# Macaron block: the attention's first layer norm takes its statistics from a summing add and a square, and one normalisation moves behind the exponentials

## The chip, the cores and the metric

The kernel runs on one core of one Trainium2 chip. The metric is the device time of one execution in microseconds (us). A core has TensorE (matmuls, PE in the profile), VectorE (DVE), ScalarE (ACT), GpSimd (POOL) and SyncE (SP), which here only issues DMAs. Each engine works through its own list in order and waits on semaphores for the others.

## The reference

The input x is (8, 1024, 512) in f32: 8192 rows of 512. Three residual blocks follow each other:

```python
x = x + 0.5 * ffn(layernorm(x), gate_w, gate_b, w1, w2)
x = x + attn(layernorm(x), Wq, bq, Wk, bk, Wv, bv, Wo, bo)
x = x + 0.5 * ffn(layernorm(x), gate_w, gate_b, w1, w2)

def layernorm(x):   # over the 512 columns
    return (x - mean(x)) / sqrt(var(x) + 1e-5)

def attn(x):        # 16 heads of 32
    q, k, v = exp(x @ Wq.T + bq), exp(x @ Wk.T + bk), x @ Wv.T + bv
    kv = cumsum(k[:, :, :, None] * v[:, :, None, :], axis=1)
    num = einsum('zsD,zsDd->zsd', q, kv)
    den = sum(q * cumsum(k, axis=1), axis=-1, keepdims=True)
    return (num / den) @ Wo.T + bo
```

ffn is a mixture of 32 experts: for each batch the gate picks the 8 rows with the highest softmax weight for every expert, merges them into one token, passes it through the expert (512 to 2048, gelu, 2048 to 512), and adds the output back at the picked rows.

## The kernel before

Rows are handled in 64 tiles of 128 rows, eight tiles to a batch. The program has three parts in time: the gate and the first ffn's 32 experts (to about 1020 us), the attention over the 64 tiles (to about 1840 us), and the second ffn's experts with the final add. During the first experts the products of the normalised input with Wq, Wk and Wv are computed ahead and stored in DRAM (p_scratch), scaled by the row's standard deviation. What the first ffn adds to a row is a combination of few expert outputs; its share in the three products is then added by a small matmul (a combination matrix MS against OS).

The change is in the attention part. Every engine's list there is a loop over n from -2 to 72, written out by hand (attention_sp, attention_pe, attention_act, attention_dve, attention_pool); in step n the tile n is live, tile m = n + 1 is prepared, and tiles n - 1 and n - 2 are finished. The steps of one tile, with the lines of the profile:

- TensorE computes for tile m four products into PSUM banks 4 to 7: the ffn's share in key, query, value (banks 4 to 6), and the ffn output itself (bank 7), semaphore s_c.
- VectorE makes X1 = x + 0.5 * bank 7 (L1133, s_x1), then adds banks 4 to 6 to the key, query and value products loaded from DRAM (PB; three adds, in the page at the helper's line L266; s_tk, s_tq, s_tv). Then it computes X1's statistics (L1139), aggregates them to mean and variance (L1141) and adds epsilon (L1143, s_x1ve).
- GpSimd raises variance plus epsilon to the power -0.5 (L1198, RS).
- ScalarE takes the exponential of the key part with scale RS (L1072), casts it to its high half KH (L1078), takes the exponential of the query part (L1080) and scales the value part (L1083). OS and the products ahead are centred, so the mean isn't needed here.
- GpSimd computes the key's low half KL (L1201), multiplies the query by exp(bias) (L1204), adds the output bias to X1 (L1207).
- TensorE adds the running sum over keys (UPTO times KH and KL, bank 2); VectorE multiplies it by the query (PR, at L266), reduces it per head (L1173) and inverts it (L1176); GpSimd multiplies the query by it (L1210).
- In the next step TensorE transposes key and query (L262); ScalarE copies them out (KT, L1060; QT, L1063); TensorE computes the scores of four heads per bank in banks 4 to 7, which have to be free for it; VectorE masks them (ST, L266); TensorE computes the attention's sums into bank 3 (s_av); ScalarE copies them out (AT, L1101) and casts the high half (ATH, L1104); GpSimd computes the low half (ATL, L1227).
- One step later TensorE does the output projection from ATH and ATL into bank 0 (s_op); VectorE adds X1 to it and sums the rows (X2, L1165, SX2); ScalarE squares it with an accumulator (L1092, SQ2); GpSimd makes scale and shift from the sums (L1217, L1220, L1222).
- One step later still ScalarE normalises X2 into XN3 (L1067, s_x2n); TensorE transposes it and ScalarE copies it (L1097); every fourth tile the gate's logits follow (ScalarE L1112). X2 is one buffer: the add L1165 of the next tile waits for XN3 of this one and for the store of X2 to DRAM.
- From tile 10 on, in every batch of eight steps, VectorE and ScalarE do the top-k of a batch (step 8k + 2: L324, L329; 8k + 3: L342, L350), TensorE and ScalarE merge its rows (L358, L365, L379), VectorE ends the merge (L392).

In step n ScalarE's order is: KT copy, QT copy, XN3 of tile n - 2, then for tile n + 1 key exponential, KH, query exponential, value scaling; top-k exponential; square of X2; copy of the transposed XN3; AT copy; ATH cast; gate logits; merge copies. TensorE waits before the scores for the two copies and for banks 4 to 7 to be read (s_x1, s_tk, s_tq, s_tv). GpSimd's rsqrt of tile n + 1 stands behind the ATL of tile n - 1.

Of the kernel before, what the change touches and what calls it, by code (L numbers as in the profile page):

```python
# [20 lines left out]
def macaron_block(nc, x, Wq, bq, Wk, bk, Wv, bv, Wo, bo, gate_w, gate_b, w1, w2, out):  # L21
# [19 lines left out]
    with ctx:  # L41
# [129 lines left out]
        SX2 = [SM[:, 228 + i:229 + i] for i in range(2)]  # L171
        SQ2 = [SM[:, 230 + i:231 + i] for i in range(2)]
        NG = NT // 4

# [3 lines left out]
        def sems(name, n):  # L178
# [26 lines left out]

        s_c, s_x1, s_tk, s_tq, s_tv, s_x1st, s_x1ag, s_x1ve, s_x1rs, s_x1b = (sem(n) for n in (
            "s_c", "s_x1", "s_tk", "s_tq", "s_tv", "s_x1st", "s_x1ag", "s_x1ve", "s_x1rs", "s_x1b"))
        s_eb, s_qb, s_qe, s_ke, s_v, s_ktT, s_kt, s_qtT, s_qt, s_S, s_st, s_av, s_at = (sem(n) for n in (
# [716 lines left out]
        def attention_pe(pe):  # L925
# [5 lines left out]
            for n in range(-2, NT + 9):  # L931
# [29 lines left out]
                if live:  # L961
                    pe.wait_ge(s_kt, n + 1)
                    pe.wait_ge(s_qt, n + 1)
                    for s_ in (s_x1, s_tk, s_tq, s_tv):
                        pe.wait_ge(s_, min(n + 2, NT))
                    for g in range(4):
                        for r in range(4):
                            R_ = slice(32 * r, 32 * r + 32)
                            t = mm(ps[:, 4 + r, 128 * g:128 * g + 128], h4(KT)[R_, g, :], h4(QT)[R_, g, :], True, True)
                            if g == 3:  # L970
                                t.then_inc(s_S, 1)
# [23 lines left out]
                if m < NT:  # L995
                    if live:
                        pe.wait_ge(s_st, 4 * n + 4)
                    b = m // 8
                    pe.wait_ge(d_ms[b % 2], 64 * (b // 2 + 1))
                    pe.wait_ge(d_os[b // 4], 16 * 16)  # L1000
                    for u in range(4):
                        t = mm(ps[:, 4 + u, :], MS[b % 2][32 * u:32 * u + 32, 128 * (m % 8):128 * (m % 8) + 128],
                               OS[b][32 * u:32 * u + 32, :], True, True)
                    t.then_inc(s_c, 1)
# [39 lines left out]
        def attention_act(act):  # L1044
# [7 lines left out]
            for n in range(-2, NT + 9):  # L1052
                live = 0 <= n < NT
                nxt = 0 <= n + 1 < NT
                m = n + 1
                gb, done = divmod(n - 10, 8)
                if live:
                    act.wait_ge(s_ktT, n + 1)
                    act.wait_ge(s_S, 4 * n)
                    nc.scalar.copy(KT, ps[:, 0, :]).then_inc(s_kt, 1)  # L1060
                    act.wait_ge(s_qtT, n + 1)
                    act.wait_ge(s_av, n)
                    nc.scalar.copy(QT, ps[:, 1, :]).then_inc(s_qt, 1)  # L1063
                if 0 <= n - 2 < NT:
                    t = n - 2
                    act.wait_ge(s_nm, t + 1)
                    nc.scalar.activation(XN3[t % NX], X2, ACT.Identity, bias=NM[t % 2],  # L1067
                                         scale=RS[2 + t % 2]).then_inc(s_x2n, 1)
                if nxt:
# [13 lines left out]
                    nc.scalar.activation(PB[m % 4][:, 2, :], PB[m % 4][:, 2, :], ACT.Identity,  # L1083
                                         scale=RS[m % 2]).then_inc(s_v, 1)
                if n >= 10 and done == 1:
                    topk_exp(act, 8 + gb)
# [32 lines left out]
        def attention_dve(dve):  # L1119
# [4 lines left out]
            for n in range(-2, NT + 9):  # L1124
# [5 lines left out]
                if nxt:  # L1130
                    dve.wait_ge(s_c, m + 1)
                    dve.wait_ge(d_x1[m % 4], 16 * (m // 4 + 1))
                    nc.vector.scalar_tensor_tensor(out=X1[m % 4], in0=ps[:, 7, :], scalar=0.5, in1=X1[m % 4],  # L1133
                                                   op0=ALU.mult, op1=ALU.add).then_inc(s_x1, 1)
                    dve.wait_ge(d_pb[m % 4], 16 * (m // 4 + 1))
                    for u, s_ in ((1, s_tk), (0, s_tq), (2, s_tv)):
                        tt(PB[m % 4][:, u, :], ps[:, 4 + u, :], PB[m % 4][:, u, :], ALU.add).then_inc(s_, 1)
                    dve.wait_ge(s_x1, m + 1)
                    nc.vector.bn_stats(ST6[m % 2], X1[m % 4]).then_inc(s_x1st, 1)  # L1139
                    dve.wait_ge(s_x1st, m + 1)  # L1140
                    nc.vector.bn_aggr(MV[m % 2], ST6[m % 2]).then_inc(s_x1ag, 1)  # L1141
                    dve.wait_ge(s_x1ag, m + 1)
                    nc.vector.tensor_scalar(VE[m % 2], MV[m % 2][:, 1:2], EPS, None, ALU.add).then_inc(s_x1ve, 1)  # L1143
                if live and c < 7:
# [41 lines left out]
        def attention_pool(pool):  # L1186
            pool.wait_ge(s_bo2, 1)
            pool.wait_ge(s_eb, 1)
            for n in range(-2, NT + 2):
                m = n + 1  # L1190
                if 0 <= m < NT:
                    j = m % 4
                    Q3 = PB[j][:, 0, :].rearrange("p (h d) -> p h d", h=16)
                    pool.wait_ge(s_x1ve, m + 1)
                    pool.wait_ge(s_atl, n)
                    for s_ in (s_ke, s_qe, s_v):
# [7 lines left out]
                    nc.gpsimd.tensor_tensor(PB[j][:, 0, :], PB[j][:, 0, :], BK, ALU.mult).then_inc(s_qb, 1)  # L1204
                    pool.wait_ge(s_x1st, m + 1)
                    pool.wait_ge(s_qb, m + 1)
# [119 lines left out]
```

## Time and profile before

| what | value |
|---|---|
| median of 3 runs | 2545.33 us (2543.61 to 2548.52) |
| profiled execution, its own time | 2545.41 us |
| its span in the trace | 2543.3 us |
| PE busy | 2106.8 us (83%) |
| VectorE busy | 855.2 us (34%) |
| ScalarE busy | 765.5 us (30%) |
| GpSimd busy | 554.0 us (22%) |
| granted TensorE clock, mean | 0.926 of full speed |

The shares are averages over the three parts. The page's forty slices are 63.6 us each; slices 17 to 29 (about 1020 to 1830 us) are the attention: there VectorE, ScalarE and GpSimd are at 4 to 7 tenths, and the DMA engines at 3 to 4 tenths, against 9 tenths in the parts before and after.

### The profile page before, as it was taken

To read this page: it belongs to the slowest core of one execution; us is meant where nothing else is said; L and a number is where in the kernel's file an instruction comes from. 1 tells how busy PE (TensorE), PEld (TensorE's weight loads), DVE (VectorE), ACT (ScalarE), POOL (GpSimd) and SP (SyncE) were. 2 spreads that over 40 slices of the span, in tenths; PEclk is the share of its full clock that TensorE was granted. 3 is DMA by queue.
4 is the path that set the end of the run, shared out by engine and by line. 5 is a ranking of instruction groups with operands and counts; after the bars stand their busy time and mean duration, and the time that the engine had idled before them with its cause. 6 is when DMAs were issued, how large, how long until landed. Compare 5 with 4: busy or idle time off the path is not lost.

```text
span 2543.3 us, 44353 instructions
## 1 busy us (share of the span) xinstructions
PE 2106.8 (83%) x18828; PEld 1228.6 (48%) x18828; DVE 855.2 (34%) x1674; ACT 765.5 (30%) x1321; POOL 554.0 (22%) x645
## 2 busy tenths in 40 slices
PE   6979999999999999888888888888766655666565
PEld 3436666666656566566666666666511111111111
DVE  6831111111111112577777677777400000000006
ACT  6722111111111112466555656656400000000000
POOL 3210000000000000566666666656300000000000
PEclk9989999999999999899999999999888887788886
DMA  9759999999999997443333333333399999999998
GB/s 361 305 200 395 397 407 407 405 413 399 412 409 405 399 395 288 177 135 114 105 113 114 120 107 118 114 105 105 143 414 424 424 423 421 423 423 425 424 424 322
DMA packets 127459, 770.23 MB, mean 303 GB/s; under 512 B 11648, under 2 KB 11648, under 8 KB 74016
## 3 DMA queue, kind: packets, MB, share of 16 engines
q1 hardware_dynamic: 118048, 717.07, 71.9%
q10 hardware_dynamic: 9216, 50.34, 4.8%
q8 instruction: 149, 2.44, 0.4%
q14 instruction: 46, 0.38, 0.0%
HBM read 660.41 MB, written 100.66 MB: 299 GB/s over the span
## 4 chain that ended last, share of the span: by engine, by line
PE 47%; DMA 32%; DVE 7%; ACT 4%; POOL 4%; issue 3%; SPq 1%; POOLq 0%; DVEq 0%; ACTq 0%
PE ps L258 44%; DMA big<-in_L_ffn_w 30%; DVE big L266 2%; PE ps L262 2%; DVE big L1253 1%; SPq L18 1%; POOL s L1201 1%; DVE big L1173 1%; POOL s L1227 1%; DMA big<-in_L_attn_x 1%; POOL big L1210 1%; ACT big L1101 1%; DMA x_scratch<-big 1%; DVE big L1133 1%; DMA xt_scratch<-big 1%
## 5 line engine op out<-in xcount | busy, mean ns | idle before, releaser
L258 PE MATMUL ps<-big 128*32 128x512 f32 (+5 forms) x13896 | 1089.0, 434 | 313.7 <-DMA big<-in_L_ffn_w 227.9
L258 PEld LDWEIGHTS ps<-big 128*32 128x32 f32 (+2 forms) x13896 | 405.4, 129 | 916.6 <-issue 527.7
L266 DVE TENSOR_TENSOR big<-ps,big 128x512 f32<-128x512 f32 (+1 forms) x565 | 340.1, 649 | 141.4 <-PE ps L258 105.3
L258 PE MATMUL ps<-wth,xth 128*128 128x512 f32 x768 | 309.0, 402 | 3.0 <-ACT big L794 3.0
L258 PE MATMUL ps<-wth,xtl 128*128 128x512 f32 x768 | 299.6, 390 | 0.0
L258 PE MATMUL ps<-wtl,xth 128*128 128x512 f32 x768 | 299.0, 389 | 0.0
L677 ACT ACTIVATE big<-ps 128x512 f32<-128x512 f32 x64 | 38.2, 597 | 836.2 <-PE ps L258 836.2
L1198 POOL TENSOR_TENSOR big<-big 128x1 f32<-128x1 f32 x64 | 35.1, 549 | 929.1 <-ACT big L1051 878.5
L701 DVE COPY big<-ps 128x128 f32<-128x128 f32 x64 | 18.3, 286 | 638.3 <-PE ps L637 638.3
L258 PE MATMUL ps<-wo,s 128*128 128x512 f32 x768 | 213.5, 431 | 1.4 <-ACT s L1104 1.4
L803 DVE TENSOR_SCALAR big<-ps,big 128x512 f32<-128x512 f32 x64 | 48.1, 751 | 403.6 <-PE ps L258 403.6
L258 PEld LDWEIGHTS ps<-wo,s 128*128 128x128 f32 x768 | 153.8, 207 | 42.0 <-ACT s L1104 1.6
L258 PEld LDWEIGHTS ps<-wth,xth 128*128 128x128 f32 x768 | 144.6, 188 | 56.1 <-issue 22.9
L262 PE MATMUL ps<-big 128*128 128x128 f32 x1032 | 146.2, 280 | 30.2 <-ACT big L474 15.5
L794 ACT ACTIVATE big<-ps,big 128x512 f32<-128x512 f32 x128 | 87.5, 688 | 240.0 <-PE ps L258 237.0
L258 PEld LDWEIGHTS ps<-wth,xtl 128*128 128x128 f32 x768 | 144.2, 188 | 31.2
L258 PEld LDWEIGHTS ps<-wtl,xth 128*128 128x128 f32 x768 | 144.4, 188 | 29.8 <-issue 1.9
L262 PEld LDWEIGHTS ps<-big 128*128 128x128 f32 x1032 | 124.1, 144 | 54.0 <-issue 23.0
L266 DVE TENSOR_TENSOR xtl<-big,xth 128x512 fp32r<-128x512 f32 x64 | 44.1, 689 | 314.6 <-ACT xth L753 314.6
L1201 POOL TENSOR_TENSOR s<-big,s 128x512 fp32r<-128x512 f32 x64 | 82.9, 1295 | 125.5 <-ACT s L1078 125.5
L258 PE MATMUL ps<-s,tri 128*128 128x512 f32 x240 | 87.4, 434 | 15.1 <-ACT s L1078 6.1
L1227 POOL TENSOR_TENSOR s<-big,s 128x512 fp32r<-128x512 f32 x64 | 86.9, 1358 | 19.8 <-ACT s L1104 14.2
(98 smaller groups left out, 1708.2 us busy)
## 6 DMA issues: line engine op xcount, KB each, us to landing
big<-in_L_ffn_w SPq DMA_DIRECT2D x256, 2048.0 KB, 17.6
p_scratch<-big ACTq DMA_DIRECT2D x64, 768.0 KB, 10.3
big<-p_scratch SPq DMA_DIRECT2D x64, 768.0 KB, 4.5
big<-in_L_attn_x SPq DMA_DIRECT2D x16, 1024.0 KB, 13.4
xt_scratch<-big SPq DMA_DIRECT2D x16, 1024.0 KB, 11.4
big<-xt_scratch SPq DMA_DIRECT2D x16, 1024.0 KB, 16.2
big<-in_L_attn_x SPq DMA_DIRECT2D x64, 256.0 KB, 2.9
x_scratch<-big SPq DMA_DIRECT2D x64, 256.0 KB, 3.2
```

The source lines that it names most:

```text
L18: return self.eng.dma_start(out, in_)
L258: return nc.tensor.matmul(o, l, r, start=start, stop=stop, skip_group_check=True)
L262: t = nc.tensor.transpose(ps[:, k, 128 * j:128 * j + 128], src[:, 128 * j:128 * j + 128], IDN[:, :])
L266: return nc.vector.tensor_tensor(o, p, q, op)
L677: nc.scalar.activation(HG[e % 2], ps[:, 0, :], ACT.Gelu).then_inc(s_hg, 1)
L794: nc.scalar.activation(PST[t % 2][:, u, :], ps[:, 2 + q % 2, :], ACT.Identity, scale=STD[:, t:t + 1]).then_inc(s_pea, 1)
L803: nc.vector.tensor_scalar(PST[t % 2][:, 2, :], ps[:, 2 + q % 2, :], STD[:, t:t + 1], None, ALU.mult).then_inc(s_ped, 1)
L1101: nc.scalar.copy(AT, ps[:, 3, :]).then_inc(s_at, 1)
L1133: nc.vector.scalar_tensor_tensor(out=X1[m % 4], in0=ps[:, 7, :], scalar=0.5, in1=X1[m % 4], op0=ALU.mult, op1=ALU.add).then_inc(s_x1, 1)
L1198: nc.gpsimd.tensor_tensor(RS[m % 2], VE[m % 2], NHALF, ALU.pow).then_inc(s_x1rs, 1)
L1201: nc.gpsimd.tensor_tensor(KL, PB[j][:, 1, :], KH.bitcast(F), ALU.subtract).then_inc(s_kl, 1)
L1227: nc.gpsimd.tensor_tensor(ATL, AT, ATH.bitcast(F), ALU.subtract).then_inc(s_atl, 1)
```

## The change

Four edits, all for the first layer norm of the attention but the last:

1. L1133's add also sums its output's rows into SX1. Statistics, aggregation and epsilon leave VectorE's list.
2. ScalarE squares (SX1 - 512 * X1) with an accumulator, SQ1; that sum over 512^3 is the variance. The output, which nobody reads, goes to PSUM bank 7. It stands first in ScalarE's step, ahead of the KT copy.
3. GpSimd makes variance plus epsilon from SQ1, one operation, ahead of the rsqrt. Its wait for the attention's low half now stands ahead of this operation.
4. ScalarE's XN3 moves from behind the QT copy to behind the value scaling.

TensorE waits before the scores for the square where it waited for the add, and again before the products of banks 4 to 7.

```diff
+        SX1 = [SM[:, 6 + 8 * i:7 + 8 * i] for i in range(2)]
+        SQ1 = [SM[:, 22 + 8 * i:23 + 8 * i] for i in range(2)]
...
@@ attention_pe
-                    for s_ in (s_x1, s_tk, s_tq, s_tv):
+                    for s_ in (s_x1sq, s_tk, s_tq, s_tv):
                         pe.wait_ge(s_, min(n + 2, NT))
...
+                    for s_ in (s_x1sq, s_tk, s_tq, s_tv):
+                        pe.wait_ge(s_, n + 2)
                     b = m // 8
@@ attention_act
+                if nxt:
+                    act.wait_ge(s_x1, m + 1)
+                    nc.scalar.activation(ps[:, 7, :], X1[m % 4], ACT.Square, bias=SX1[m % 2], scale=-float(D),
+                                         accum_out=SQ1[m % 2]).then_inc(s_x1sq, 1)
                 if live:
                     act.wait_ge(s_ktT, n + 1)
...
-                if 0 <= n - 2 < NT:
-                    t = n - 2
-                    act.wait_ge(s_nm, t + 1)
-                    nc.scalar.activation(XN3[t % NX], X2, ACT.Identity, bias=NM[t % 2],
-                                         scale=RS[2 + t % 2]).then_inc(s_x2n, 1)
                 if nxt:
                     act.wait_ge(s_tk, m + 1)
...
                     act.wait_ge(s_tv, m + 1)
                     nc.scalar.activation(PB[m % 4][:, 2, :], PB[m % 4][:, 2, :], ACT.Identity,
                                          scale=RS[m % 2]).then_inc(s_v, 1)
+                if 0 <= n - 2 < NT:
+                    t = n - 2
+                    act.wait_ge(s_nm, t + 1)
+                    nc.scalar.activation(XN3[t % NX], X2, ACT.Identity, bias=NM[t % 2],
+                                         scale=RS[2 + t % 2]).then_inc(s_x2n, 1)
@@ attention_dve
-                                                   op0=ALU.mult, op1=ALU.add).then_inc(s_x1, 1)
+                                                   op0=ALU.mult, op1=ALU.add,
+                                                   accum_out=SX1[m % 2]).then_inc(s_x1, 1)
...
-                    dve.wait_ge(s_x1, m + 1)
-                    nc.vector.bn_stats(ST6[m % 2], X1[m % 4]).then_inc(s_x1st, 1)
-                    dve.wait_ge(s_x1st, m + 1)
-                    nc.vector.bn_aggr(MV[m % 2], ST6[m % 2]).then_inc(s_x1ag, 1)
-                    dve.wait_ge(s_x1ag, m + 1)
-                    nc.vector.tensor_scalar(VE[m % 2], MV[m % 2][:, 1:2], EPS, None, ALU.add).then_inc(s_x1ve, 1)
@@ attention_pool
+                    pool.wait_ge(s_x1sq, m + 1)
+                    pool.wait_ge(s_atl, n)
+                    nc.gpsimd.tensor_scalar(VE[m % 2], SQ1[m % 2], 1.0 / D ** 3, EPS, ALU.mult,
+                                            ALU.add).then_inc(s_x1ve, 1)
                     pool.wait_ge(s_x1ve, m + 1)
-                    pool.wait_ge(s_atl, n)
...
-                    pool.wait_ge(s_x1st, m + 1)
                     pool.wait_ge(s_qb, m + 1)
```

## Rows read from the trace of the kernel before

**Rows 1.** Busy time by stretch, tiles 30 to 37 (eight): us, PE, PEld, DVE, ACT, POOL busy, clock, DMA.
```profile
1395.85:1495.06 99.21, 87.23 (x1343) 64.39 (x1342) 73.26 (x144) 59.79 (x109) 63.60 (x73) 0.97 0.37 113
```

**Rows 2.** Who waited for whom, 1200 to 1790 us: total us, times, longest us.
```profile
ACT big L1072 <- POOL big L1198: 59.2, 30, 3.9
...
PE ps L258 <- DVE big L266: 40.4, 18, 3.3
POOL big L1198 <- DVE big L1143: 39.3, 18, 3.0
...
DVE big L266 <- POOL big L1204: 20.1, 20, 1.8
...
PE ps L258 <- ACT big L1063: 11.3, 30, 0.5
ACT big L1060 <- PE ps L262: 10.1, 18, 0.7
```

**Rows 3.** Groups of instructions by shape, 1180 to 1790 us: busy us, mean ns.
```profile
L1067 ACT ACTIVATE big<-big 128x512 f32<-128x512 f32 x50 | 41.0, 820 | 0.8
...
L1092 ACT ACTIVATE big<-big 128x512 f32<-128x512 f32 x49 | 35.4, 722 | 62.7 <-DVE big L1165 62.3
...
L1139 DVE BATCH_NORM_STATS2 big<-big 128x6 f32<-128x512 f32 x50 | 34.1, 681 | 0.0
...
L1217 POOL TENSOR_SCALAR big<-big 128x1 f32<-128x1 f32 x49 | 13.8, 282 | 9.4 <-POOL big L1210 9.4
```

**Rows 4.** Timeline, tiles 31 to 32: start us, us, engine, line; idle before in brackets.
```profile
1422.44 0.69 DVE L1165 SCALAR_TENSOR_TENSOR big<-ps,big 128x512 f32<-128x512 f32 x1 [2.02 <-PE ps L258]
...
1423.17 0.72 ACT L1092 ACTIVATE big<-big 128x512 f32<-128x512 f32 x1 [2.28 <-DVE big L1165]
...
1423.89 0.56 ACT L1097 COPY big<-ps 128x512 f32<-128x512 f32 x1
...
1427.07 0.62 ACT L1104 CAST s<-big 128x512 fp32r<-128x512 f32 x1
1427.59 0.58 ACT L1060 COPY big<-ps 128x512 f32<-128x512 f32 x1
...
1428.07 0.59 ACT L1063 COPY big<-ps 128x512 f32<-128x512 f32 x1
...
1428.76 1.17 PE L258 MATMUL ps<-big 32*128 32x128 f32 x32 [0.45 <-ACT big L1063]
...
1429.81 0.72 ACT L1072 ACTIVATE big<-big 128x512 f32<-128x512 f32 x1 [0.45 <-POOL big L1198]
...
1431.72 0.71 ACT L1083 ACTIVATE big<-big 128x512 f32<-128x512 f32 x1
...
1434.10 0.69 DVE L266 TENSOR_TENSOR big<-ps,big 128x512 f32<-128x512 f32 x1 [0.49 <-POOL big L1204]
```

**Rows 5.** Timeline, tile 33.
```profile
1443.29 0.19 PEld L258 LDWEIGHTS ps<-s,tri 128*128 128x128 f32 x1 [0.99 <-POOL s L1201]
```

**Rows 6.** Timeline, tile 34.
```profile
1456.86 0.69 DVE L266 TENSOR_TENSOR big<-ps,big 128x512 f32<-128x512 f32 x1 [0.33 <-POOL big L1204]
```

**Rows 7.** Timeline, tiles 35 and 36.
```profile
1462.42 0.69 DVE L1133 SCALAR_TENSOR_TENSOR big<-ps,big 128x512 f32<-128x512 f32 x1
...
1465.05 1.24 PE L258 MATMUL ps<-big 32*128 32x128 f32 x32 [3.35 <-DVE big L266]
...
1477.94 1.17 PE L258 MATMUL ps<-big 32*128 32x128 f32 x32 [1.31 <-DVE big L266]
...
1482.33 0.19 PEld L258 LDWEIGHTS ps<-s,tri 128*128 128x128 f32 x1 [0.45 <-POOL s L1201]
```

**Rows 8.** Busy time and granted clock by stretch, tiles 35 and 36.
```profile
1465.05:1470.70 5.65, 5.65 (x45) 4.58 (x46) 3.52 (x8) 3.81 (x6) 3.02 (x3) 0.70 0.01 3
1477.94:1482.30 4.36, 4.36 (x45) 3.34 (x45) 3.70 (x9) 2.59 (x4) 1.85 (x2) 1.00 0.08 29
```

**Rows 9.** Timeline, tile 4.
```profile
1081.42 0.69 DVE L1165 SCALAR_TENSOR_TENSOR big<-ps,big 128x512 f32<-128x512 f32 x1 [5.92 <-DMA x_scratch<-big]
```

More of the change, by code:

```diff
@@ L204, in macaron_block @@
             "s_ost", "s_oag", "s_oc", "s_ocT", "s_och", "s_ocl", "s_ow", "s_os"))
-        s_c, s_x1, s_tk, s_tq, s_tv, s_x1st, s_x1ag, s_x1ve, s_x1rs, s_x1b = (sem(n) for n in (
-            "s_c", "s_x1", "s_tk", "s_tq", "s_tv", "s_x1st", "s_x1ag", "s_x1ve", "s_x1rs", "s_x1b"))
+        s_c, s_x1, s_tk, s_tq, s_tv, s_x1sq, s_x1ve, s_x1rs, s_x1b = (sem(n) for n in (
+            "s_c", "s_x1", "s_tk", "s_tq", "s_tv", "s_x1sq", "s_x1ve", "s_x1rs", "s_x1b"))
         s_eb, s_qb, s_qe, s_ke, s_v, s_ktT, s_kt, s_qtT, s_qt, s_S, s_st, s_av, s_at = (sem(n) for n in (
```

## The prediction

> **What bounds the kernel now.** The table by slices places the attention part between about 1030 and 1830 us; nothing outside it is touched. The views by stretch come next. Eight tiles take 99.21 us, in which TensorE is busy 87.23, VectorE 73.26, ScalarE 59.79 and GpSimd 63.60 [rows 1]. No engine is full, so the tile's period (12.4 us) is a loop through all of them, and busy time taken from VectorE is worth nothing by itself. The waits say which loop closes where. TensorE waits for VectorE before the score matmuls 18 times in some 49 tiles (40.4 us), and for ScalarE's query copy (L1063) in 30 tiles, 11.3 us in all [rows 2]. So in three of eight tiles VectorE's four adds release the scores, and in the other five the copies on ScalarE do, by a small margin each. A second loop goes through GpSimd: rsqrt (L1198), key exponential (L1072), key split, query product, and then VectorE's product with the running sum; that product waits for GpSimd's L1204 20 times, 20.1 us [rows 2].
>
> The timeline of tile 32 shows the first loop: after the matmuls of attention end, ScalarE does the split copy ATH at 1427.07, the key copy at 1427.59, the query copy at 1428.07, and the scores start at 1428.76, released by it [rows 4]. These instructions stand back to back.
>
> I follow one period (tiles 32 to 39, where the number modulo 8 decides which top-k and merge work lies beside) and write down how late each event comes.
>
> **The change, part by part.**
>
> *Removed from VectorE:* the statistics, 0.681 a tile [rows 3], and two operations on a column or six. They stood behind the three adds that free the banks for the scores, so no score start waits for them. What waited is the rsqrt: 18 times, 39.3 us [rows 2]. These are the tiles whose adds come late (35, 36, 39). There rsqrt and key exponential now come up to 1.7 us earlier, since the square needs the first add alone, but in 35 and 39 the end is set by scores, output projection and the X2 add, not by the key's path. In tile 36, where the key's path does end last, GpSimd's attention split ahead of the rsqrt comes 1 us late by the ledger below, about where the statistics ended, so little is won. I take 0.
>
> *The summing add:* L1133 gets the accumulator that L1165 has. That one takes 0.69 [rows 4], as the L1133 that starts after a wait does [rows 7]; its sum is there 0.73 after its start (1422.44 to 1423.17 [rows 4]). I take 0 for VectorE; bounds 0 and 0.08.
>
> *The square on ScalarE:* the same form as L1092, 0.722 [rows 3], and the next instruction starts 0.72 after it (1423.17 to 1423.89 [rows 4]). It stands ahead of the key copy, hence in the loop that releases the scores. Queued behind it are key copy, query copy, key exponential; behind these wait the scores, and GpSimd. No row shows ScalarE writing its output to PSUM. By the nearest rows a slot lies between 0.48 (key copy to query copy, both from PSUM [rows 4]) and 0.82 (L1067 [rows 3]); I take 0.72, the row with the same operation and accumulator.
>
> The Trainium skill (ScalarE: Activation LUTs, "Step-by-step: what each stage is for") says that ScalarE reaches PSUM with less latency than SBUF, and recommends PSUM as a destination; the square writes its unused output there. By that rule the slot would be under 0.72; with 0.6 as an estimate the sum below would be about 7 instead of 8.4. L1092, with an SBUF output, cannot show it.
>
> Where the adds are late the square runs beside them: from the add's start 0.73 to the sum, 0.72 square, 0.48 key copy, 0.69 query copy to scores is 2.62; before, add start to scores was 2.63 (1462.42 to 1465.05 [rows 7]). So tiles 35, 36 and 39 pay nothing. In the others ScalarE pays 0.72, less what it idled before the key copy anyway: 18 waits, 10.1 us [rows 2], mean 0.56.
>
> *Variance on GpSimd:* one more small operation ahead of the rsqrt, of L1217's kind, 0.282 with its gap hidden [rows 3]: 0.27 on GpSimd's loop a tile. Bounds: 0.19 and 0.64 (what a small power operation such as L1198 occupies, by its 0.55 and a gap). It waits for the square and the attention split; behind it in GpSimd's queue is the whole key path.
>
> *XN3 behind the value scaling:* ScalarE's order alone. The exponential can start up to 0.82 [rows 3] earlier where XN3 stood in its way; in 30 tiles the exponential waited for GpSimd regardless (59.2 us [rows 2]), so there nothing is won. New is that X2's buffer is free only after XN3, and XN3 stands behind the value scaling (L1083), which starts 1.91 after the exponential, 1429.81 to 1431.72, and takes 0.71 [rows 4]: XN3 ends 1.91 + 0.71 + 0.82 = 3.44 after the exponential's start. The product on VectorE follows GpSimd 4.29 after it (1434.10 [rows 4]), so an X2 add of 0.69 still fits ahead, by some 0.15. The top-k transposition, however, waits for XN3 about 0.4 in tile 33. DMAs: SP's loads and the X2 store follow the X2 add and shift with it; none was waited for in steady tiles.
>
> **The ledger of a period**, us late against before. Scores of 32: 0.72. Its product waited for GpSimd with 0.49 to spare [rows 4], and GpSimd is 0.27 late: product 0.27, attention end 0.72. Tile 33: scores 0.72 more, less 0.13 idle: 1.3. GpSimd 0.54. TensorE's weight load had sat 0.99 waiting for the key split [rows 5]; I give back 0.4 of it: end 0.9. Tile 34: 0.72 less an idle of 0.3: scores 1.3; the product had 0.33 to spare [rows 6], so it is 1.0 late, and with it the top-k work and the adds. Tile 35: 1.0. Tile 36: scores 1.0, end 1.0 less the 0.45 waited for the key split [rows 7]: 0.55. Tile 37: the merge's transposition makes ScalarE idle, the square fits in: 0.55. Tile 38: 0.72 less 0.4 idle: 0.9. Tile 39: 0.9, by the adds. The next period begins 0.9 late: 0.9 for eight tiles.
>
> Seven periods (tiles 8 to 63): 6.3. At tile 4 the X2 add waits 5.92 for the store of the tile before, behind the three expert loads [rows 9]; that swallows what came earlier but for the slip of those loads' issue, 0.3. Tiles 5, 6, 7 pay 0.72, 0.4, 0.7: 1.8. Behind tile 63 no square is left. Sum 8.4. The second expert stage starts from attention's end, all of it lands. The profiled execution took 2545.41 (span 2543.3), 0.1 from the median 2545.33: so 2553.7.
>
> **Rivals.**
>
> *A, not slower: GpSimd's path is what really ends each tile.* Place: the key exponential. If the square disappears in ScalarE's idle time (40% of the stretch [rows 1]) and only XN3's departure counts, tiles 34 and 38 win 0.3 to 0.8 on the product, against 0.54 from the variance: about -0.3 a period, -2 in all: 2543.4. It decides if the scores have over 0.7 to spare. For it: 20 waits for L1204, with 1.0 each. Against: spare time of 0.49 and 0.33, and the 30 releases by L1063.
>
> *B, slower still: the clock falls more often.* After TensorE sat 3.35 idle its clock was granted at 0.70 in tile 35 (a mix of 1.2 and 2.4 GHz); after 1.31 in tile 36 it was 1.00, and the same stretch to the end of the projection took 5.65 against 4.36 [rows 7, 8]. The square lengthens idle before the scores in tiles 32 and 33 from 0.45 to 1.2 or 1.4. If one of these tips, 1.3 a period is added: about 9, 2563.
>
> *C: the variance costs its upper bound* (0.64): product of 33 1.28 late, of 34 past its spare: 0.4 to 0.6 more a period, 2557.
>
> That the change does not do what it says: the arithmetic is complete in the diff, no chance set aside.
>
> **Numbers.** Forecast 0.62 (own range 2550 to 2557, by a slot of 0.6 to 0.82), A 0.24, B 0.08, C 0.06. Range 2545 to 2562: A is mostly left out, B nearly at its edge. A measurement tells 0.2% (5.1 us) from nothing. Slower: forecast 0.56, B and C 0.14: 0.70. Within: 0.06 of the forecast and 0.14 of A: 0.20. Faster: the rest of A, 0.10.
>
> **What would show it.** The square at 0.72 and its successor 0.72 behind; scores released by L1063's counterpart after longer waits (about 1.1 in 32) and VectorE idle more; eight tiles at about 100.1; GpSimd's product releases unchanged in number or fewer; tiles 35, 36, 39 with 2.6 from add to scores. Wrong if eight tiles take 99.2 or less, if the square takes under 0.5, or if stretches of clock 0.70 come more than twice in a period.

## The result, and the profile after

The changed kernel takes 2557.0 us (median of 20 runs, 2546.8 to 2567.4) against 2547.8 for the one before (20 runs, 2541.5 to 2553.2). The ratio is 1.0038, 95% interval [1.0025, 1.0051]: 9.2 us slower by the medians, where 8.4 was forecast. The same kernel sent again later gave 1.0050 [1.0033, 1.0066], 8 runs. The spread of single runs is as large as the effect, so most of what follows is read from one measure: the time from one attention copy (AT) to the next, which gives the length of each tile's step.

The profiled execution of the changed kernel was its slowest (span 2565.4). Its first attention copy comes 6.1 us later than before, and all of that lies ahead of the attention, where nothing is changed; in the second profile of the same kernel it comes 0.3 earlier (1048.2 against 1048.6). It is no part of the effect.

Stretches of eight tiles, 24 to 32, from copy to copy, in the kernel after (us; busy time of PE, PEld, DVE, ACT, POOL with counts; granted clock, DMA share, GB/s):

```profile
1352.49:1452.85 100.36, 86.76 (x1339) 64.78 (x1340) 65.63 (x130) 65.37 (x125) 64.82 (x81) 0.97 0.37 112
```

and the same tiles before:

```profile
1336.97:1435.92 98.95, 87.25 (x1339) 64.42 (x1340) 73.25 (x144) 59.79 (x108) 63.37 (x73) 0.97 0.36 112
```

VectorE lost 7.6 us of work in eight tiles, ScalarE got 5.6 and GpSimd 1.4 more, and the stretch is 1.41 us longer at the same clock.

Who waited for whom after, 1200 to 1800 us (total us, times, longest), against [rows 2]:

```profile
PEld ps L260 <- ACT big L1068: 67.9, 42, 3.0
PE ps L260 <- ACT big L1071: 66.0, 48, 3.0
...
ACT big L1075 <- POOL big L1204: 21.8, 24, 1.9
...
ACT ps L1063 <- DVE big L1141: 18.7, 12, 1.7
DVE big L1168 <- ACT big L1091: 12.9, 12, 1.6
...
DVE big L268 <- POOL big L1210: 0.4, 1, 0.4
```

(L1068 and L1071 are the key and the query copy, L1075 the key exponential, L1063 the square, L1141 the summing add, L1168 the X2 add, L1091 XN3, L1210 GpSimd's query product.) The scores now wait for ScalarE's query copy in every one of 48 tiles, 66 us in all, where VectorE's adds ended 18 of these waits and the copy 30, 52 us together. X2 waits for XN3 in 12 tiles, a wait that was not there. VectorE's product waits for GpSimd 0.4 us instead of 20.1, but only a part of this is slack won on GpSimd's path: with the square alone (the experiment below) the wait is 11.4 us, with XN3 in its old place 7.3 (both 1200 to 1790 us), and the rest is hidden by the X2 add, which stands ahead of the product and now waits for XN3.

The new operations (busy us, mean ns, 1180 to 1790 us), against [rows 3]:

```profile
L1091 ACT ACTIVATE big<-big 128x512 f32<-128x512 f32 x49 | 39.3, 801 | 0.0
...
L1063 ACT ACTIVATE ps<-big 128x512 f32<-128x512 f32 x48 | 33.2, 691 | 19.1 <-DVE big L1141 18.7
...
L1199 POOL TENSOR_SCALAR big<-big 128x1 f32<-128x1 f32 x48 | 9.1, 190 | 29.5 <-ACT ps L1063 25.7 <-POOL s L1232 3.8
...
L1063 ACT ACTIVATION_READ_ACCUMULATOR ps<-big 128x1 f32 x48 | 9.1, 189 | 0.1
```

Tile 32 in the kernel after, against [rows 4]: attention copy, split copy, square, key copy, query copy, scores.

```profile
1442.66 0.59 ACT L1109 COPY big<-ps 128x512 f32<-128x512 f32 x1 [2.00 <-PE ps L260]
...
1443.28 0.62 ACT L1112 CAST s<-big 128x512 fp32r<-128x512 f32 x1
1443.81 0.69 ACT L1063 ACTIVATE ps<-big 128x512 f32<-128x512 f32 x1
...
1444.53 0.56 ACT L1068 COPY big<-ps 128x512 f32<-128x512 f32 x1
...
1444.99 0.58 ACT L1071 COPY big<-ps 128x512 f32<-128x512 f32 x1
...
1445.67 1.17 PE L260 MATMUL ps<-big 32*128 32x128 f32 x32 [1.15 <-ACT big L1071]
```

From the split copy to the scores it is 2.39 us, before 1.69 (1427.07 to 1428.76): 0.70 more. TensorE's idle before the scores is 1.15 instead of 0.45.

The steps of one period, at equal clock, are the main table of this document. A step is the difference of two starts of the attention copy; each number is the median over tiles 17 to 61 with that number modulo 8, with steps 3 and 7 taken where the mean clock was 0.88 or 0.89 and the others where it was 1.00.

| kernel | 0 | 1 | 2 | 3 | 4 | 5 | 6 | 7 | sum | against before |
|---|---|---|---|---|---|---|---|---|---|---|
| before | 9.47 | 11.47 | 12.45 | 14.66 | 11.63 | 11.81 | 13.04 | 14.42 | 98.94 | |
| after | 10.18 | 11.65 | 13.07 | 14.41 | 11.35 | 11.80 | 13.44 | 14.43 | 100.33 | +1.39 |
| after, again | 10.18 | 11.65 | 13.07 | 14.25 | 11.35 | 11.79 | 13.47 | 14.41 | 100.18 | +1.24 |
| after, XN3 in its old place | 10.18 | 11.37 | 13.08 | 14.40 | 11.34 | 11.79 | 13.47 | 14.42 | 100.06 | +1.11 |
| after, statistics kept too | 10.17 | 11.67 | 13.07 | 14.50 | 11.35 | 11.81 | 13.47 | 14.41 | 100.45 | +1.50 |
| before, square only | 10.18 | 11.19 | 13.07 | 14.53 | 11.64 | 11.81 | 13.47 | 14.41 | 100.30 | +1.35 |
| before, variance only | 9.56 | 11.96 | 12.45 | 14.66 | 11.92 | 11.80 | 13.05 | 14.42 | 99.81 | +0.87 |
| before, XN3 moved only | 9.55 | 11.69 | 12.44 | 14.45 | 11.93 | 11.79 | 13.05 | 14.39 | 99.29 | +0.35 |
| square moved early | 9.85 | 12.08 | 12.41 | 14.40 | 11.34 | 11.80 | 13.05 | 14.41 | 99.35 | +0.40 |
| ... and XN3 back | 9.58 | 12.38 | 12.42 | 14.56 | 11.36 | 11.79 | 13.03 | 14.40 | 99.52 | +0.58 |
| ... and no variance step | 9.49 | 11.87 | 12.41 | 14.39 | 11.35 | 11.80 | 13.03 | 14.41 | 98.75 | -0.20 |
| hybrid | 9.47 | 11.46 | 12.45 | 14.76 | 11.45 | 11.80 | 13.04 | 14.54 | 98.97 | +0.03 |
| hybrid, XN3 late in step 2 | 9.47 | 11.46 | 12.46 | 14.80 | 11.45 | 11.79 | 13.05 | 14.54 | 99.02 | +0.08 |

Steps 3 and 7 rest on one to six samples each. Step 3 rests on a single one in the second profile of the changed kernel, with the statistics kept, with the square early, and with XN3 back; single tiles of this place differ by up to 0.55 at nearly the same clock (14.38 to 14.93 before), so small differences there mean nothing. The 14.25 of the second profile is tile 43, which is short in the kernel before too (14.38). Tile by tile, the changed kernel's step 3 is 0.25 shorter in tile 27 and 0.26 in tile 59.

### The profile page after: what moved, and what is told of

Read it like the earlier page. It is cut to its first block, busy times and chain, and to the rows that moved or that the text cites. A ratio compares the mean times of both kernels' runs of the same rounds, so it can differ in the third digit from the quotient of the medians.

```text
span 2565.4 us, 44355 instructions
## 1 busy us (share of the span) xinstructions
PE 2113.4 (82%) x18828; PEld 1234.3 (48%) x18828; DVE 795.4 (31%) x1546; ACT 809.8 (32%) x1449; POOL 565.7 (22%) x709
## 4 chain that ended last, share of the span: by engine, by line
PE 50%; DMA 30%; ACT 8%; DVE 5%; issue 4%; POOL 2%; SPq 1%; POOLq 0%; DVEq 0%; ACTq 0%
PE ps L260 47%; DMA big<-in_L_ffn_w 29%; PE ps L264 2%; DVE big L1258 1%; SPq L18 1%; ACT ps L1063 1%; ACT big L1068 1%; ACT big L1071 1%; ACT big L1109 1%; ACT big L1120 1%; DVE big L268 1%; DVE big L1176 1%; DMA xt_scratch<-big 1%; DMA x_scratch<-big 1%; PE ps L639 1%
## 5 line engine op out<-in xcount | busy, mean ns | idle before, releaser
L260 PE MATMUL ps<-big 128*32 128x512 f32 (+5 forms) x13896 | 1100.4, 437 | 335.1 <-DMA big<-in_L_ffn_w 227.7
L260 PEld LDWEIGHTS ps<-big 128*32 128x32 f32 (+2 forms) x13896 | 411.2, 131 | 944.7 <-issue 480.9
L1199 POOL TENSOR_SCALAR big<-big 128x1 f32<-128x1 f32 x64 | 12.2, 190 | 919.9 <-ACT ps L1063 914.5
```

Source lines behind the costliest of these rows:

```text
L260: return nc.tensor.matmul(o, l, r, start=start, stop=stop, skip_group_check=True)
```

## The experiments

Theory S: the square stands in the loop that releases the scores, and costs there. Rival G: GpSimd's path sets the end of each tile, and the variance operation is the cost. The table above has the steps.

**The changed kernel again.**

> The changed kernel once more. My ledger, corrected by its first trace: at equal clock eight tiles (tile 24 to 32 and the like) take about 1.4 us more than before, by steps +0.7 (tile 32), +0.2, +0.6, -0.25, -0.3, 0, +0.4, 0; 7 to 11 us in all. Theory S (the square stands in the loop that releases the scores) and rival G (GpSimd's path with the variance is what costs) both give this; the run is the base for the next three. If the 6 us by which the first tile's attention came late in the first trace are noise of the part before, they are smaller or absent here.

Ratio 1.0050. The steps repeat to 0.03 us, except step 3. The late first tile is gone.

**XN3 in its old place.** The diff is against the changed kernel.

```diff
                     nc.scalar.copy(QT, ps[:, 1, :]).then_inc(s_qt, 1)
+                if 0 <= n - 2 < NT: ... XN3 ...
...
                                          scale=RS[m % 2]).then_inc(s_v, 1)
-                if 0 <= n - 2 < NT: ... XN3 ...
```

> The changed kernel with XN3 back behind the query copy. Theory S: XN3 behind the value scaling costs TensorE 0.2 to 0.4 in tiles 33 and 36 (it waits for XN3 before the transposition) and wins nothing where the X2 add is last, so eight tiles take 0.3 to 0.6 us less than the changed kernel, 2 to 4 in all: about 1.0025 of before. Rival G: the key exponential starts 0.5 to 0.8 later in five tiles and each tile ends later, so 2 to 5 us more than the changed kernel.

Ratio 1.0026 [1.0010, 1.0042], 12 runs. Step 1 is 0.28 shorter. The medians show no other difference, but in the six tiles of step 3 that can be paired at the same mean clock with one of the changed kernel's two profiles, this kernel takes between 0.02 less and 0.35 more, 0.1 on average. So moving XN3 was a small loss in this kernel, taken in tile 33 and in part given back in tile 35; the 0.3 expected in tile 36 isn't there. G's 2 to 5 us more did not come.

**The square alone**, added to the kernel before with the statistics kept. TensorE waits for it as in the change, and GpSimd's add of the output bias to X1 waits for it too (not shown):

```diff
+                if nxt:
+                    act.wait_ge(s_x1, m + 1)
+                    nc.scalar.activation(ps[:, 7, :], X1[m % 4], ACT.Square, bias=HALF, scale=-float(D),
+                                         accum_out=SM[:, 22 + 8 * (m % 2):23 + 8 * (m % 2)]).then_inc(s_x1sq, 1)
                 if live:
                     act.wait_ge(s_ktT, n + 1)
```

> The kernel before, its statistics kept, with a square of X1 into PSUM bank 7 ahead of the key copy; nobody uses its sum, the scores wait for it. Theory S: eight tiles 0.9 to 1.4 us more than before, 6 to 10 us in all, nearly the whole of the change. Rival G: under 0.4 us per eight tiles, under 3 in all.

Ratio 1.0060 [1.0037, 1.0082], 6 runs. Its eight tiles 24 to 32:

```profile
1353.53:1453.86 100.33, 86.82 (x1339) 64.84 (x1340) 73.01 (x144) 65.07 (x124) 63.25 (x73) 0.97 0.36 112
```

The square by itself gives 100.33, the changed kernel 100.36. Steps 0, 2 and 6 are those of the changed kernel to 0.03.

**The variance alone**, one more small operation ahead of the rsqrt in the kernel before:

```diff
                     pool.wait_ge(s_atl, n)
+                    nc.gpsimd.tensor_scalar(SM[:, 22 + 8 * (m % 2):23 + 8 * (m % 2)], VE[m % 2], 1.0 / D ** 3, EPS,
+                                            ALU.mult, ALU.add).then_inc(s_x1va, 1)
+                    pool.wait_ge(s_x1va, m + 1)
```

> The kernel before with one more small operation on GpSimd ahead of the rsqrt, whose result nobody uses. Theory S: 0.27 a tile on GpSimd, on the path only in tiles 32, 33 and partly 36, so 0.2 to 0.6 us per eight tiles, 1 to 4 in all. Rival G: 0.27 in each tile, 2.2 per eight, 15 in all; with the upper bound of 0.64 still more.

Ratio 1.0043 [1.0028, 1.0058], 10 runs. Eight tiles:

```profile
1349.28:1449.11 99.83, 87.34 (x1339) 64.46 (x1340) 73.01 (x143) 59.75 (x109) 64.86 (x80) 0.97 0.36 113
```

This is 0.87 a period, more than S said and less than half of G's 2.2. It falls on step 1 (0.49) and step 4 (0.29), the two in which TensorE waited for the key split before, and 0.09 on step 0. So G is right in two tiles of eight. By steps the sum over 56 tiles is 6 us; the ratio's 11 stands above that, its lower end (7) near it. In this run's profile the first attention copy comes 8.9 us later than before (1057.4 against 1048.6), ahead of anything that was changed, so part of the 11 may be no effect of the edit; this was not tested.

**XN3 alone**, moved in the kernel before as in the change.

> The kernel before with XN3 alone behind the value scaling. Theory S: TensorE finds XN3 later in tile 33 (about 0.3 more in its interval, as the 0.29 between the changed kernel and the one with XN3 in its old place) and in 36 (0.3), and the key exponential's earlier start wins about 0.3 in tile 35's interval: -0.1 to +0.4 per eight tiles at equal clock, within 3 us of before in all. Rival G: the exponential's earlier start is a gain in each tile, over 0.8 per eight tiles, 6 us less than before.

Ratio 1.0005 [0.9993, 1.0017], 12 runs. Steps 1 and 4 pay 0.22 and 0.30, step 3 wins 0.2 (TensorE waits for XN3, the exponential starts earlier), +0.35 in all, as S had it. Taken singly, the three additions come to 1.35 + 0.87 + 0.35 = 2.57 a period, the whole change to 1.39. In steps 0 and 1 they come to 1.31 singly and 0.89 in the change: there they lengthen loops that run side by side. The larger part lies in step 4, 0.60 singly and -0.28 in the change. The change has a fourth part which none of the three has: the rsqrt takes its input from the square and not from the statistics.

**The square early.** In four of eight steps the square goes to the end of the step before, where ScalarE idles for TensorE:

```diff
+            def early(m):
+                return 2 <= m < NT and (m - 2) % 8 in (1, 4, 5, 7)
...
-                if nxt:
-                    (square of m)
+                if nxt and not early(m):
+                    square1(m)
...
+                if early(n + 2):
+                    square1(n + 2)
                 if live:
                     act.wait_ge(s_av, n + 1)
```

> The changed kernel with the square moved: in four of eight steps (1, 4, 5, 7) it stands at the end of the step, ahead of the attention copy, where ScalarE idles for TensorE; in the other four it stays ahead of the key copy, three of which wait for the adds anyway. Theory S: the steps of tiles 32, 34 and 38 fall back to those of before (9.5, 12.5, 13.0 us), what is left is 0.2 to 0.5 us per eight tiles from GpSimd and XN3: 2 to 4 us in all. Rival G: the square's place changes nothing, 1.2 to 1.4 per eight.

Ratio 1.0014 [1.0002, 1.0025], 12 runs. Nothing is left out of the computation here, only an instruction has another place, and 1.0 of 1.39 us a period is gone: steps 2 and 6 are back at 12.4 and 13.05, step 0 at 9.85. Step 1 got 0.4 longer. In tile 33 the attention copy follows right behind the early square, about 0.1 late, but the other 0.3 is GpSimd's: the tile before ended 0.33 earlier (step 0), the key split did not move with it, and from the scores to the attention matmuls it takes 5.75 instead of 5.42 (1448.56 to 1454.31; after 1455.86 to 1461.28). G's "the place changes nothing" is refuted.

**Early, and XN3 back** behind the query copy in all steps but step 2.

> The same as the kernel with the square moved, and XN3 back behind the query copy but in step 2 of eight. Theory S: per eight tiles -0.3 to +0.2 us at equal clock, within 2.5 us of before in all. Rival G: as the one before it, with 0.5 more for XN3.

Ratio 1.0018 [1.0004, 1.0032], 12 runs. A miss: 0.58 a period where -0.3 to 0.2 was expected. Step 1 went up by another 0.3, as step 0 went down by 0.27. The trace of tile 33 shows where:

```profile
1453.36 0.69 DVE L268 TENSOR_TENSOR big<-ps,big 128x512 f32<-128x512 f32 x1 [1.48 <-POOL big L1223]
...
1455.65 0.69 ACT L1054 ACTIVATE ps<-big 128x512 f32<-128x512 f32 x1 [2.19 <-DVE big L1154]
...
1456.37 0.57 ACT L1122 COPY big<-ps 128x512 f32<-128x512 f32 x1
```

VectorE's product waits 1.48 for GpSimd's query product, the summing add (L1154) stands behind it, the early square (L1054) waits for that add, and the attention copy (L1122) for the square. From the attention matmuls' start (1452.77) to the copy it is 3.60, with the square early alone 3.31, in the changed kernel 3.22 (1461.28 to 1464.50). So GpSimd's path reaches the attention copy through the early square.

**Early, XN3 back, and no variance operation.** The weights are scaled by 512^1.5 when they are transposed, the rsqrt takes the sum of squares itself; epsilon is left out of the attention's first norm.

```diff
-                nc.scalar.copy(WTH[m][:, kt, :] if m < 3 else WO[:, kt, :], ps[:, 2 + u % 2, :]).then_inc(s_wth, 1)
+                nc.scalar.activation(WTH[m][:, kt, :] if m < 3 else WO[:, kt, :], ps[:, 2 + u % 2, :], ACT.Identity,
+                                     scale=float(D ** 1.5) if m < 3 else 1.0).then_inc(s_wth, 1)
...
-                    nc.gpsimd.tensor_tensor(RS[m % 2], VE[m % 2], NHALF, ALU.pow).then_inc(s_x1rs, 1)
+                    nc.gpsimd.tensor_tensor(RS[m % 2], SQ1[m % 2], NHALF, ALU.pow).then_inc(s_x1rs, 1)
```

> The same with the variance operation on GpSimd gone: the weights are scaled by 512^1.5 when they are transposed, and the rsqrt works on the sum of squares itself; epsilon is left out. Theory S: per eight tiles 0.5 to 0.9 us less than before at equal clock (GpSimd's 0.27 a tile gone, and the key exponential of tile 36 no longer behind VectorE's statistics), 3 to 6 us less in all. If the clock falls of tile 35 decide more than these steps, the total does not show it.

Ratio 1.0008 [0.9995, 1.0021], 12 runs; eight tiles:

```profile
1338.11:1436.86 98.75, 86.78 (x1339) 64.62 (x1340) 65.70 (x128) 65.43 (x125) 63.45 (x73) 0.97 0.38 113
```

Taking 0.27 from GpSimd's path shortens step 1 by 0.51 and the period by 0.78: below the kernel before by 0.20, less than half of what was expected. The total can't tell it from before; in this profile the clock also fell in tiles 18 and 50, where it stays up in nearly all other profiles.

**The statistics kept** in the changed kernel, unused:

```diff
+                    nc.vector.bn_stats(ST6[m % 2], X1[m % 4]).then_inc(s_x1st, 1)
...
+                    nc.vector.bn_aggr(MV[m % 2], ST6[m % 2]).then_inc(s_x1st, 1)
...
+                    nc.vector.tensor_scalar(MV[m % 2][:, 0:1], MV[m % 2][:, 1:2], EPS, None, ALU.add).then_inc(s_x1st, 1)
```

> The changed kernel with the three statistics operations put back on VectorE behind its adds; their result is not used, the rsqrt still comes from the square. Theory S: VectorE's freed 1.0 us a tile is worth nothing, the steps stay those of the changed kernel within 0.1 us each (10.2, 11.65, 13.1, 14.4 at a clock of 0.88, 11.35, 11.8, 13.45). Rival V (the freed VectorE time wins part of the step of tile 36): that step goes back from 11.35 to 11.63.

Ratio 1.0028 [1.0014, 1.0041], 12 runs. With 7.6 us of VectorE work put back in every eight tiles, no step moves by more than 0.1: the freed time was worth nothing. For step 3 the best evidence is at a mean clock of 1.00: 12.96 to 12.99 in tiles 19, 27 and 35 and 12.65 in tile 43 here, 12.97 to 12.99 and 12.66 in the changed kernel's two profiles. Step 4 stays 11.35, so its gain comes from where the rsqrt gets its input, not from a free VectorE.

**Hybrid:** the kernel before, with square and variance only for tiles 0, 4 and 5 modulo 8, whose adds come late.

```diff
+        def squared(m):
+            return 12 <= m < NT and m % 8 in (0, 4, 5)
...
-                if nxt:  (statistics on VectorE)
+                if nxt:  (statistics on VectorE if not squared(m))
...
+                if nxt and squared(m):
+                    act.wait_ge(s_x1, m + 1)
+                    (square, as in the change)
```

> The kernel before, with the square, the summing add and the variance on GpSimd only for the tiles whose number modulo 8 is 0, 4 or 5 (from 12 on), where VectorE's adds come late; the others keep the statistics on VectorE; XN3 in its old place. Theory S: the squares stand beside the adds and cost nothing, the key exponential of tile 37 comes a microsecond earlier: the interval that ends with tile 36 is 11.35 instead of 11.63, the rest as before: -0.3 per eight tiles, 2 us less than before, less than 0.1%, which the total hardly shows. Rival G: 0.27 more in each of these tiles.

> The same with XN3 behind the value scaling in step 2 of eight alone. Theory S: the key exponential of tile 35 comes earlier, the interval that ends with tile 35 is 0.15 to 0.3 shorter at equal clock: -0.45 to -0.6 per eight tiles, 3 to 4 us less than before in all.

Ratios 0.9996 [0.9984, 1.0007] and 0.9994 [0.9982, 1.0006], 11 and 12 runs. Both are within noise of before: step 4 is 0.18 shorter, steps 3 and 7 are 0.1 longer, and TensorE's idle before the scores is 0.12 longer in steps 3, 4 and 7 (3.05 to 3.17, 1.31 to 1.43, 2.39 to 2.51), so here the squares beside the adds were not free; why they are in the changed kernel and not here was not traced. XN3 late in step 2 wins nothing (14.80 against 14.76), where 0.15 to 0.3 was expected. They beat the changed kernel; that they beat the kernel before is not shown.

## Why the prediction was right, point by point

**The direction and the mechanism held.** The forecast was that the square enters the loop that releases the scores and that VectorE's freed time buys nothing. One term of it, tile 36's, had another cause than forecast (below). The square alone gives as long a period as the whole change, moving it into idle time takes most of it back, and putting the statistics back changes nothing.

**The ledger, step by step** (forecast by its own differences, then measured in the changed kernel):

| step | 0 | 1 | 2 | 3 | 4 | 5 | 6 | 7 | sum |
|---|---|---|---|---|---|---|---|---|---|
| forecast | +0.72 | +0.2 | +0.1 | 0 | -0.45 | 0 | +0.35 | 0 | +0.9 |
| measured | +0.71 | +0.18 | +0.62 | -0.25 | -0.28 | -0.01 | +0.40 | +0.01 | +1.39 |

The ledger let tile 34's end stand at 1.0, that of its product, though its scores stood at 1.3. The end in fact follows the scores, and 0.25 is given back in step 3, where the adds, released by the product, set the pace: this is a matter of where a delay is booked. What is really mis-sized is two terms, and one of them had the wrong cause.

*Tile 34's slot.* I let 0.3 of the 0.72 vanish in idle time. Tile 26 of the kernel after (same place in the period; square, its accumulator read, key copy, scores):

```profile
1366.93 0.69 ACT L1063 ACTIVATE ps<-big 128x512 f32<-128x512 f32 x1
...
1367.63 0.20 ACT L1063 ACTIVATION_READ_ACCUMULATOR ps<-big 128x1 f32 x1
...
1367.86 0.59 ACT L1068 COPY big<-ps 128x512 f32<-128x512 f32 x1
...
1369.03 1.17 PE L260 MATMUL ps<-big 32*128 32x128 f32 x32 [0.97 <-ACT big L1071]
```

Before (tile 26 too: key copy, query copy):

```profile
1351.23 0.59 ACT L1060 COPY big<-ps 128x512 f32<-128x512 f32 x1
...
1352.02 0.58 ACT L1063 COPY big<-ps 128x512 f32<-128x512 f32 x1 [0.20 <-PE ps L262]
```

The key copy starts 0.93 behind the square, not 0.72. What is given back lies between the two copies: 0.79 before, 0.48 after, so 0.31, as the ledger had it. That leaves 0.62.

*Tile 36's gift.* I booked the 0.45 that the weight load had waited for the key split, because TensorE would come later to it. The split is used by the second of two matmuls. Both, and that weight load, in tile 28 before (same place in the period), then the two matmuls after:

```profile
1382.69 0.92 PE L258 MATMUL ps<-s,tri 128*128 128x512 f32 x2
...
1383.11 0.19 PEld L258 LDWEIGHTS ps<-s,tri 128*128 128x128 f32 x1 [0.46 <-POOL s L1201]
```

```profile
1398.78 0.62 PE L260 MATMUL ps<-s,tri 128*128 128x512 f32 x2
```

The wait is gone after, but the matmuls got only 0.30 shorter: a weight load idles while TensorE is still busy with the matmul before it, so its 0.45 was not TensorE's. The cause was wrong as well. With the square alone the scores come later too, and the wait stays as it was (0.45, the two matmuls 0.92, step 4 11.64), since rsqrt still waits for the statistics. With the statistics put back but unused it is gone (0.62, step 4 11.35). So the 0.28 comes from the rsqrt's new input, the term that the prediction took at 0 for tile 36, and not from TensorE's delay. XN3 and the variance have no part in what is missing: step 4 is 11.35 also where XN3 is back and the variance operation gone.

*Tile 33* came out as booked. Of its two parts, the scores were to be 0.59 later (0.72 less 0.13) and the weight load to give 0.4 back; from the attention copy before to the scores it is 0.57 more, and from the scores to the attention matmuls 0.38 less. With the square alone 0.83 is given back there; GpSimd's variance and XN3 take the rest. TensorE's wait for XN3, which the prediction saw:

```profile
1460.69 0.42 PEld L264 LDWEIGHTS ps<-big 128*128 128x128 f32 x4 [0.38 <-ACT big L1091]
```

The X2 add waits for XN3 as well, in tile 33 and, without cost by the steps, in tile 28:

```profile
1460.84 0.69 DVE L1168 SCALAR_TENSOR_TENSOR big<-ps,big 128x512 f32<-128x512 f32 x1 [1.33 <-ACT big L1091]
...
1399.21 0.69 DVE L1168 SCALAR_TENSOR_TENSOR big<-ps,big 128x512 f32<-128x512 f32 x1 [0.76 <-ACT big L1091]
```

The run with XN3 back has step 1 0.28 shorter and step 4 unchanged (11.34).

**The summing add** cost VectorE nothing, as forecast: in tile 33 the next add starts 0.55 behind it in both kernels (1435.71 to 1436.26 before, 1452.24 to 1452.79 after).

**Tiles 35, 36 and 39 pay nothing: held.** Summing add to scores, tile 27 after, against [rows 7]: 1379.35 to 1381.99, 2.64 us; 2.63 before.

```profile
1379.35 0.69 DVE L1141 SCALAR_TENSOR_TENSOR big<-ps,big 128x512 f32<-128x512 f32 x1
...
1381.99 2.09 PE L260 MATMUL ps<-big 32*128 32x128 f32 x32 [2.93 <-ACT big L1071]
```

The releaser is another (the query copy for the adds), the moment the same.

**The variance on GpSimd** was priced well as an operation, 0.19 long and 0.27 to its successor. Tile 33 of the kernel after:

```profile
1456.40 0.19 POOL L1199 TENSOR_SCALAR big<-big 128x1 f32<-128x1 f32 x1 [0.16 <-POOL s L1232]
1456.67 0.55 POOL L1204 TENSOR_TENSOR big<-big 128x1 f32<-128x1 f32 x1
```

Its effect was underrated: alone it costs 0.87 a period, where 0.2 to 0.6 was expected in the run's text and rival A took GpSimd to gain. How much of it is left in the changed kernel no run shows, as none takes it out there; with the square early and XN3 back, taking it out gives 0.78.

**Rival A** (not slower, GpSimd's path decides) failed at the point it named: the scores had no 0.7 to spare in tiles 32, 34 and 38. **Rival C** (the variance at its upper bound) fell with the 0.27. **Rival B** (more clock falls) came true at a place that I had not named, tile 7. Scores and output projection there, second profile of the changed kernel, then before:

```profile
1122.97 1.17 PE L260 MATMUL ps<-big 32*128 32x128 f32 x32 [2.05 <-ACT big L1071]
1124.07 4.61 PE L260 MATMUL ps<-wo,s 128*128 128x512 f32 x12
```

```profile
1121.76 1.17 PE L258 MATMUL ps<-big 32*128 32x128 f32 x32 [1.35 <-ACT big L1063]
1122.87 3.01 PE L258 MATMUL ps<-wo,s 128*128 128x512 f32 x12
```

The idle before the scores grew from 1.35 to 2.05 by the square, and the twelve projection matmuls take 4.61 instead of 3.01 at a mean clock of 0.87 in the tile instead of 1.00. Every profile of a kernel with a square in every tile shows it but one: with the square early, XN3 back and no variance operation, the idle is the same and the matmuls take 3.03 (step 7 is 11.20 at a mean clock of 1.00):

```profile
1121.95 1.17 PE L260 MATMUL ps<-big 32*128 32x128 f32 x32 [2.05 <-ACT big L1080]
1123.05 3.03 PE L260 MATMUL ps<-wo,s 128*128 128x512 f32 x12
```

The kernels with no square there don't show it. So the longer idle goes with the fall and does not by itself decide it. It costs 1.6 us once, not once a period. The first profile of the changed kernel, and the one with the statistics kept, have a second fall in tile 6 (14.4 us at 0.88, where the second profile has 12.9 at 1.00). In tiles 32 and 33 (idle 1.15 after) the clock stayed at 1.00.

**The signs.** Eight tiles at about 100.1 came out as 100.36. The sign of being wrong, 99.2 or less, would have misled: in the second profile the same stretch takes 98.91, because its tile 27 ran at a mean clock of 1.00 (12.97 us) and not 0.88 (14.43).

**The sum.** Seven periods of 1.39 are 9.7 us; tiles 1 to 7 took 84.49 us in the second profile against 81.38: 3.1, of which the ledger had 2.1 with the slip. That is about 12.9, and the attention from first to last copy took 13.2 longer (781.43 against 768.22). The parts agree less well: tiles 8 to 63 took 10.1 longer in the second profile and 8.7 in the first, tiles 1 to 7 4.8 in the first. The totals moved by 9.2 and 12.1 in the two sets of runs. So the forecast of 8.4 was low by its steps, 0.9 a period for 1.39, and near the first measurement partly by luck. What lies between 12.9 and 9.2 was not traced; the clock of tile 35's kind, below, differs from run to run by as much.

## What to carry to other kernels

Ask of an added instruction which waiting engine is released by what stands behind it in its own queue, not how busy its engine is: 0.7 us on an engine that idled 40% cost 0.71, 0.62 and 0.43 in three tiles of eight, and nothing in the other five. Ask the same of a removed one: 7.6 us of VectorE's time in eight tiles were worth nothing, while taking the rsqrt's input from another place won 0.28. An idle of the weight load isn't an idle of TensorE: 0.46 of the one was 0.30 of the other. When several loops run close together, costs don't add: in steps 0 and 1 three edits cost 1.31 one by one and 0.89 in the change. When runs scatter as widely as the effect, compare step lengths at equal clock; seven of eight repeated to 0.03 us.

## What the runs showed of the hardware that was not expected

The square into PSUM lasts 0.691 us, the square into SBUF 0.722 [rows 3]; the Trainium skill (ScalarE: Activation LUTs, "Step-by-step: what each stage is for") says PSUM is the lower-latency destination, and the duration agrees. The next instruction still starts 0.72 later (1443.81 to 1444.53), as it did behind the square into SBUF, so the slot was not shorter; it was 0.93 in tile 26 and in most others of its place in the period, and 0.83 in tile 29 and its like.

The steps of tiles 3 modulo 8 come in three lengths, 13.0, 14.4 and 15.7 us at a mean granted clock of 1.00, 0.88 and 0.78, with about 3 us of idle ahead of the scores in all of them (2.6 to 3.5). Most kernels show more than one of the three. The two profiles of the changed kernel have two tiles each at 1.00 in place of 0.88 (tiles 35 and 43, and 19 and 27), and one or two more at 0.78. In step 7 the three kernels with the early square have 12.84 at a clock of 1.00 in four, three and two of five tiles, where before and after have 14.4 at 0.88 in nearly all, with the same 2.4 us of idle ahead of the scores. What decides the clock there was not tried; it moves a run by several us and is the likeliest source of the spread among runs.
